# A two-layer transformer on one core: table stores for all batches at once, and 16-bit queries and keys written by ScalarE

## What is computed

```python
x = x + attn0(layernorm(x))   # 16 heads of 8, relative position bias, gated
x = x + ffn0(layernorm(x))    # 16 experts, 4 used per token, and shared experts
x = x + attn1(layernorm(x))   # 8 heads
x = x + ffn1(layernorm(x))    # 4-bit quantised
```

```python
q, k, v = split_heads(h @ Wq.T + bq), split_heads(h @ Wk.T + bk), split_heads(h @ Wv.T + bv)
pos_bias = transpose(rel_embed[buckets], (2, 0, 1))
gate_out = gate_a * (gate_b * gru_const - 1.0) + 2.0      # per token and head
scores = einsum('bhid,bhjd->bhij', q, k) / sqrt(8) + gate_out * pos_bias
out = softmax(scores) @ v
```

## Time and profile before

| | us |
|---|---|
| median of 3 runs | 2229.55 (2228.36 to 2238.91) |
| profiled execution, its own time | 2230.54 |
| its span, first to last instruction | 2228.7 |
| TensorE busy in the span | 1991.5 |
| VectorE busy | 1618.8 |
| ScalarE busy | 1343.3 |
| GpSimd busy | 1107.5 |

### The profile page before, as it was taken

One profiled execution on the slowest core, in us unless ns is written; L12 is line 12 of the kernel. 1 busy time (PEld: TensorE's weight loads), 2 busy tenths in 40 slices (PEclk: granted clock), 3 DMA queues, 4 the chain that ended last, 5 costly groups with the idle time before them and its releaser, 6 DMA issues. The chain is left out here.

```text
span 2228.7 us, 56143 instructions
## 1 busy us (share of the span) xinstructions
PE 1991.5 (89%) x17787; PEld 1012.5 (45%) x17787; DVE 1618.8 (73%) x3426; ACT 1343.3 (60%) x2148; POOL 1107.5 (50%) x994
## 2 busy tenths in 40 slices
PE   4788999999999999995599979999999999999775
PEld 3534444444444444445244424444444444444444
DVE  4977888888888888866677766566656666667896
ACT  2245666666666666663355547777877777778421
POOL 1432322222233222234254538777877778778565
PEclk7779999999999999997799979999999999999897
DMA  5621222112222211100012341111111111110000
GB/s 132 187 54 47 54 53 51 50 50 51 53 53 53 53 51 50 50 24 1 1 48 75 110 127 29 44 29 29 43 29 29 43 29 29 43 29 2 0 15 24
DMA packets 127064, 107.24 MB, mean 48 GB/s; under 512 B 39636, under 2 KB 102724, under 8 KB 126956
## 3 DMA queue, kind: packets, MB, share of 16 engines
q1 hardware_dynamic: 120544, 99.83, 16.9%
q10 hardware_dynamic: 6412, 6.18, 1.0%
HBM read 76.01 MB, written 29.53 MB: 47 GB/s over the span
## 5 line engine op out<-in xcount | busy, mean ns | idle before, releaser
L1103 DVE TENSOR_REDUCE b_mx<-psum 128x1 f32<-128x512 f32 x1024 | 664.0, 686 | 148.6 <-PE psum L920 83.4
L1087 ACT ACTIVATE b_prob<-psum 128x1024 f32<-128x1024 f32 x512 | 524.4, 1024 | 327.2 <-PE psum L952 327.1
L1917 POOL TENSOR_TENSOR combT<-attn,f_phi 128x512 f16<-128x512 f32 x512 | 587.0, 1157 | 182.0 <-ACT f_phi L2051 152.4
L2072 DVE TENSOR_REDUCE f_mx<-psum 128x1 f32<-128x512 f32 x512 | 328.6, 683 | 170.1 <-PE psum L1941 169.8
L2050 ACT ACTIVATE attn<-psum 128x512 f32<-128x512 f32 x512 | 308.0, 602 | 176.2 <-PE psum L1952 167.0
L1000 PE MATMUL psum<-b_prob,combT 128*32 128x256 f32 x4096 | 329.1, 393 | 1.5 <-ACT b_prob L1087 0.5
L852 POOL COPY combT<-v 128x64 f32 (+1 forms) x64 | 15.7, 246 | 604.4 <-PE psum L1000 594.8
L2051 ACT ACTIVATE f_phi<-psum 128x512 f16<-128x512 f32 x512 | 306.2, 598 | 0.0
L952 PE MATMUL psum<-x,b_toep 128*128 128x79 f16 (+1 forms) x4224 | 268.4, 208 | 0.0
L952 PEld LDWEIGHTS psum<-x,b_toep 128*128 128x128 f16 x4224 | 236.7, 99 | 9.3 <-issue 2.6
L855 POOL TENSOR_TENSOR x<-flip,grev 128x1024 f16<-128x1024 f16 x128 | 240.7, 1901 | 0.0
(11 more groups left out here) (321 smaller groups left out, 3391.4 us busy)
## 6 DMA issues: line engine op xcount, KB each, us to landing
f_qk<-d_qk SPq DMA_DIRECT2D x192, 128.0 KB, 2.9
d_qk<-e_qk SPq DMA_DIRECT2D x64, 256.0 KB, 2.6
b_toep<-d_line SPq DMA_DIRECT2D x128, 64.0 KB
b_q<-d_q SPq DMA_DIRECT2D x128, 54.0 KB
d_k<-a_qk SPq DMA_DIRECT2D x48, 128.0 KB, 2.3
b_toep<-d_line SPq DMA_DIRECT2D x128, 32.0 KB
b_q<-b_m SPq DMA_DIRECT2D x256, 1.0 KB
b_q<-d_q SPq DMA_DIRECT2D x128, 27.0 KB
```

The source lines that it names most:

```text
L1087: nc.scalar.activation(prob[:, t % 4, :].rearrange("p (a n) -> p a n", a=2), ps[:, EXP + 2 * (t % 2):EXP + 2 * (t % 2) + 2, :], ACT.Exp).t ...
L1103: nc.vector.tensor_reduce(mx[:, b, t, half:half + 1], ps[:, bank, :], AX.X, ALU.max).then_inc(s.max_read, 1)
L1917: nc.gpsimd.tensor_tensor(plo[:, t % 4, at], prob[:, t % 4, at], phi[:, t % 4, at], ALU.subtract).then_inc(s.plo_ready, 1)
L2072: nc.vector.tensor_reduce(mx[:, b, t, half:half + 1], ps[:, bank + half, :], AX.X, ALU.max).then_inc(s.max_read, 1)
```

## The change

Two parts.

1. The stores of the far constants cover all four batches in one DMA each, with the batch as a repeated dimension of the source. For each side x the rows 24, 25 and 26 are one store of 128 KB each: 6 stores for 16. SyncE's last wait of the phase follows (1 + 6 stores).
2. In the projection ScalarE does each of query and key twice from PSUM, once into `qk32` and once into the high part of `qk16`, in 16 bits, and raises `q_biased` and `k_biased` after the second. VectorE's casts and the link behind them go, and L593 of the query stands directly behind the wait for the query. Since ScalarE now writes `qk16`, it waits for `stored[u]` of chunk n-2 ahead of the query's activation; VectorE keeps its own wait. `LINKS` becomes 3.

```diff
@@ phase_weights, SyncE @@
                 for x in range(2):
-                    for b in range(B):
-                        tok = slice(b * N, (b + 1) * N)
-                        sp.dma_start(g.d_k[x, :, 3 * D0:3 * D0 + 2, tok], farw[:, x, 0:1, :].to_broadcast([H0, 2, N])).then_inc(tab_stored, 16)
-                        sp.dma_start(g.d_k[x, :, 3 * D0 + 2, tok], farw[:, x, 1, :]).then_inc(tab_stored, 16)
-                sp.wait_ge(tab_stored, 16 * (1 + 4 * B))
+                    for row, part in enumerate((0, 0, 1)):
+                        sp.dma_start(g.d_k[x, :, 3 * D0 + row, :].rearrange("h (b n) -> h b n", b=B),
+                                     farw[:, x, part:part + 1, :].to_broadcast([H0, B, N])).then_inc(tab_stored, 16)
+                sp.wait_ge(tab_stored, 16 * (1 + 6))
@@ phase_project0 @@
-    LINKS = 4
+    LINKS = 3
@@ phase_project0, ScalarE @@
             act.wait_ge(s.qk_parts, done(n - 2))
+            act.wait_ge(stored[u], 16 + (n - u) * (11 * 16 // 2))
             act.wait_ge(s.q_psum, done(n))
-            nc.scalar.activation(qk32[:, u, 0, :], ps[:, Q, :], ACT.Identity, bias=g.bqk[:, 0:1], scale=float(SCALE0)).then_inc(s.q_biased, 1)
+            nc.scalar.activation(qk32[:, u, 0, :], ps[:, Q, :], ACT.Identity, bias=g.bqk[:, 0:1], scale=float(SCALE0))
+            nc.scalar.activation(qk16[:, u, 0, 0, :], ps[:, Q, :], ACT.Identity, bias=g.bqk[:, 0:1], scale=float(SCALE0)).then_inc(s.q_biased, 1)
             act.wait_ge(s.k_psum, done(n))
-            nc.scalar.activation(qk32[:, u, 1, :], ps[:, K, :], ACT.Identity, bias=g.bqk[:, 1:2]).then_inc(s.k_biased, 1)
+            nc.scalar.activation(qk32[:, u, 1, :], ps[:, K, :], ACT.Identity, bias=g.bqk[:, 1:2])
+            nc.scalar.activation(qk16[:, u, 1, 0, :], ps[:, K, :], ACT.Identity, bias=g.bqk[:, 1:2]).then_inc(s.k_biased, 1)
             if not last:
                 move_xT(n + 1, 1 - u)
@@ phase_project0, VectorE @@
             dve.wait_ge(stored[u], 16 + (n - u) * (11 * 16 // 2))
             for i, ready in enumerate((s.q_biased, s.k_biased)):
                 dve.wait_ge(ready, done(n))
-                ins = nc.vector.tensor_copy(qk16[:, u, i, 0, :], qk32[:, u, i, :])
-            link(ins)
-            for i in range(2):
                 ins = nc.vector.tensor_tensor(qk16[:, u, i, 1, :], qk32[:, u, i, :], qk16[:, u, i, 0, :], ALU.subtract)
             ins.then_inc(s.qk_parts, 1)
```

## The result

The changed kernel takes 2208.5 us (median of 17 runs, 2199.6 to 2227.5), the kernel before in the same comparison 2224.9 us (17 runs, 2217.9 to 2270.4). The ratio is 0.9928, 95% interval [0.9906, 0.995]: 16 us faster where 4.4 were forecast, and under the lower end of the range. The profiled execution of the changed kernel spans 2216.8 us and took 2218.6 us.

What follows compares the result with a forecast made beforehand. TensorE was taken to bound attention 0, with the change touching only the first 108 us. From 2230.5 us, 3.6 for the table stores and 0.8 for the projection gave 2226.1 us, range 2219 to 2232.

Steps and rivals of the forecast that it cites:

- The step that failed: After attention 0's first product at 108.54 us: everything later only shifts by whatever the first 108 us gain.
- Part one: Weights phase: six table stores instead of sixteen start the next phase at 33.6 instead of 37.2 us, 3.6 us off.
- the third rival: Weights phase: larger table stores drain late, so part one gives nothing or costs a microsecond; 2229.7 to 2231 us, chance 0.15.
- the late end: Weights phase: table stores at 178 GB/s plus one landing finish at 33.6 us, leaving a gain of 2.6 us.
- Part two, the mechanism: Projection: ScalarE waits for chunk n-2's stores to land and becomes the bound; VectorE's saved 0.79 us becomes a wait.
- The landing: Projection: time for the gates' store L491 to land, taken as 2.3 us from a range of 1.4 to 3.1.
- The four activations: Projection, ScalarE: four activations per chunk at 0.57 us each, two of them added at a cost of 1.14 us.
- the 2.99 us from L476 to the gates' store: Projection, ScalarE: fixed part of a round from the transposed chunk's copy to L491, giving rounds of 5.37 us plus landing.
- Part two, the sum: Projection: 0.3 us gained by L364 of chunk 7 plus 0.5 us in the last chunk, 0.8 us in all.
- the first rival: Projection: landing stays short at 1.4 us, rounds 6.77 us; 9.1 us gained with the table's 3.6, 2221.4 us, chance 0.25.
- what would prove me wrong altogether: Attention 0, 144 to 940 us: it should neither grow nor shrink itself, being TensorE's.

Runs made afterwards that it cites:

- run 1: Kernel before plus only ten increments of an unused semaphore on ScalarE ahead of attention 1; 2205.5 us, ratio 0.9926.
- run 2: Changed kernel plus 118 increments of an unused semaphore, putting ScalarE's attention 1 loop at instruction 958; 2232.1 us, ratio 1.0032.
- run 4: Kernel before with only the second part, activations on ScalarE and VectorE's casts gone; 2207.3 us, ratio 0.9932.
- run 7: Changed kernel with the far tables built on and stored from 128 partitions, same six stores and bytes; 2203.7 us, ratio 0.9913.
- run 6: Changed kernel with the gates' two stores counted apart, so only VectorE waits for them; 2206.8 us, ratio 0.9919.
- run 8: Changed kernel with both the gates' stores counted apart and the far tables stored from 128 partitions; 2205.5 us, ratio 0.985.
- run 5: Kernel before with 60, 112 or, last, 86 unused increments on ScalarE ahead of attention 1; 2205.5 us (0.992), 2214.8 us (0.9968), last one's time unreadable.

## Why the prediction was wrong

- **The step that failed** is the sentence that what follows the first product of attention 0 "only shifts, as it waits for nothing of fixed date". I looked for waits and found none. But ScalarE's program of attention 1 was itself late in every turn, and how late depended on its place in the instruction memory, which each instruction added ahead of it moves. Runs 1 and 2 show it both ways: the shift without the change gives 0.9926, the change without the shift 1.0032. The place made the whole of the difference that the runs can measure. That the kernel came out faster, as forecast, is luck: in the profiles 16.8 us came from a stage that the sum left out and 0.9 from the two that it costed. The profile of before did show the fault: five transfers in each turn on the instruction queue of ScalarE, waits "issue" on L2050, one long item in four. I had read attention 0 for even work and never read attention 1.
- **Part one, mis-sized**: 3.6 us forecast, -0.1 us measured (10.3 against 10.4 us), as in the third rival. I had taken the issue (0.465 us a store) to set the rate of the sixteen, and a rate of the projection's stores, 178 GB/s, as the late end. The time went by the bytes: the stores of the tables ran at 97 GB/s from 27 to 34.5 us before, at 99 after. The 74 GB/s of the row that I had for them held their idle ends too, so it was the right row with too low an average.
- **Part two, the mechanism**: the waits came as written in some rounds, on ScalarE for the landing (1.3 to 2.1 us) and on VectorE for the 16-bit half (up to 1.5), and not in all four. The landing was well sized, 2.6 us in the median against 2.3. The four activations were too: 2.30 us against 2.28. The term that failed is the 2.99 us from L476 to the gates' store, taken as fixed. In run 2 that distance is 3.35, 1.48, 2.29, 1.42 and 2.17 us, because the stores are issued while the copy still waits or runs: in the round of the 1.48 the first two of them, at 59.82 and 60.59 us, are ahead of the copy at 61.19. A round is then 6.4 us, VectorE's own, and not 7.67.
- **Part two, the sum**: 0.8 us forecast. The profiled execution gave 0.5, and its second to fourth rounds of 7.20, 7.38 and 8.48 us average 7.7, as forecast. That is half luck. In the second and the fourth VectorE stood 0.6 and 1.9 us for the 16-bit halves, behind ScalarE's 1.25 and 1.63 us for the gates' store: my mechanism. In the third ScalarE waited 1.41 us for TensorE's query product instead. The granted clock was 0.72, 0.82 and 0.83 in the three, but it isn't shown to be their cause: runs 4 and 7 have such a round at the full clock, run 6 has rounds of 6.49 us at 0.75 and 0.82. In run 2, where no round was long, the projection took 66.1 us, 5.2 less than the 71.3 of before; the other kernels with this part took 67.3 to 67.6, those without it 71.3 to 71.7. So this part is worth about 4 us, nearer to the first rival (5.5) than to the forecast. In the timed runs it is lost in their scatter.
- **Attention 0** grew by 4.1 us in the profiled execution, which I had named as what would prove me wrong altogether. It comes from the same family of causes as attention 1 (below), not from the change: it takes 870.2 us in run 4 with ScalarE's part and 870.0 in run 1 without.

## What to carry to other kernels

Before costing a change to a long program, look at the instruction queues' transfers by time, at "issue" among the waits, and at the distance from item to item in every loop, also far from the edit: a loop that is fetched anew each turn costs microseconds that any edit ahead of it can take or give. To judge an edit, add the same number of empty instructions to the kernel before and compare with that. And take a store's rate from stores of the same shape: fewer instructions save nothing where the bytes set the time.

## What the hardware showed that I had not expected

- **ScalarE's loop of 18 KB** stays in the instruction memory at places 20, 72 and 122 in steps of 128 instructions, and is fetched in five transfers of 8 KB each turn at 46 and 62. Each jump back then has 2.39 to 2.75 us between branch and next instruction (four kernels, at 46 and 62 alike), against 0.24 to 0.26 in the others. From the first L2036 to the last it cost 17.6 us at place 62 (725.6 against 708.0 us in the kernel with 60 increments) and 7.8 us at place 46 (715.8).
- **TensorE has the like in attention 0**, and there it changes from run to run. In some of the first turns one item of four takes 19 to 21 us instead of 13.5, and TensorE's queue q8 (16 KB a transfer) makes nine transfers more for each. TensorE's wait in the kernel of run 8 from 120 to 400 us:

```profile
PE psum L947 <- issue: 13.9, 3, 5.0
```

  Its page has three such items and 60 transfers; run 1 has none and 33:

```profile
q8 instruction: 60, 0.98, 0.2%
```

```profile
q8 instruction: 33, 0.54, 0.1%
```

  In the twelve profiles here with 0, 1, 2, 3 or 6 such items the count is 33, 42, 51, 60 or 87: 33 and nine for each. The profiled execution of before has one (6.4 us over 13.5), that of the changed kernel two (11.5 us together), which is more than the 4.1 us by which its attention 0 is longer. One costs 5.5 to 7.4 us, and six of them made run 5's last profile 2246 us long. Much of the scatter of all the times here, 2199 to 2227 us for the changed kernel, is probably this. What decides how many turns pass until the loop stays was not tried and is open.
- **VectorE slows beside GpSimd again**: while GpSimd builds the diagonals, the two operations L592 of a chunk took 2.98 us together instead of 1.29, the like of what L364 and L590 show in the earlier trace rows.
